# Spectral resampling, channel MLP and a selective scan on one core: TensorE work of the next sample moved and paired

## The reference

```python
def conv_ref(x, W1, b1, W2, b2, coef):      # layer 0
    xu = _upsample_rfft(xc)                 # band-limited, 64x64 -> 128x128
    h = h @ W1.T + b1                       # 96 -> 384 channels
    h = coef[:, 0] + coef[:, 1] * h + coef[:, 2] * (h * h)
    h = h @ W2.T + b2                       # 384 -> 96
    return _lpf_rfft(hc)[:, :, ::2, ::2]    # low pass, back to 64x64
...
def mamba(u, ...):                          # layer 1, L = 4096 steps in time
    xs, z = split(u @ W_in.T)               # 2 x 192 channels
    xc = silu(causal conv of 3 taps of xs)
    delta = softplus(dt @ W_dt.T + b_dt)    # dt, B, C = xc @ W_x.T
    h = exp(delta * A) * h + delta * B * xc # h: 192 channels x 16 states
    y = (h . C + xc * D) * silu(z)
    return y @ W_out.T
x = x + conv_ref(_gn(x), ...)
x = x + mamba(_gn(x), ...)
```

## Time and profile before

| what | us |
|---|---|
| median of 3 runs | 6282.98 (6277.81 to 6292.53) |
| the profiled execution, its own time | 6281.37 |
| its span, first to last instruction | 6279.6 |
| TensorE busy (modelled ends) | 6000.8, 96% of the span |
| VectorE busy | 5683.0, 90% |
| GpSimd busy | 5215.4, 83% |
| ScalarE busy | 5094.3, 81% |
| share of the 16 DMA engines' span | 66.3% |

### The profile page before, as it was taken

The page is one execution under the profiler, slowest core; times in us unless marked ns, Lnnn a source line. Parts: engine busy times, 40 slices in busy tenths (PEclk is TensorE's granted clock), DMA queues, the critical chain, the costliest instruction groups (busy, mean ns, idle before and its releaser), DMA issues. The chain is left out here.

```text
span 6279.6 us, 99521 instructions
## 1 busy us (share of the span) xinstructions
PE 6000.8 (96%) x32251; PEld 3116.7 (50%) x32251; DVE 5683.0 (90%) x4450; ACT 5094.3 (81%) x8658; POOL 5215.4 (83%) x5092
## 2 busy tenths in 40 slices
PE   8999999999999999999999999999999999998776
PEld 5645545454554545555455555545455454544222
DVE  0089999999999999999999999999999999999998
ACT  4588888888888888888888888888888888887664
POOL 0078888888888888888888888888888888888887
PEclk9999999999999999999999999999999999998665
DMA  3367676676767667676776767667676766766553
GB/s 95 89 167 174 161 172 155 168 166 165 172 156 169 158 168 169 160 180 145 173 162 161 175 156 180 150 167 166 163 171 163 171 158 164 167 147 157 131 118 75
DMA packets 805829, 983.27 MB, mean 157 GB/s; under 512 B 391259, under 2 KB 417543, under 8 KB 805319
## 3 DMA queue, kind: packets, MB, share of 16 engines
q1 hardware_dynamic: 805318, 976.92, 66.3%
HBM read 717.71 MB, written 259.00 MB: 156 GB/s over the span
## 5 line engine op out<-in xcount | busy, mean ns | idle before, releaser
L1183 POOL TENSOR_TENSOR hc<-hs,cs 128x512 f32<-128x512 f32 x3072 | 3840.8, 1273 | 631.0 <-DVE hs L1142 486.7
L1142 DVE TENSOR_TENSOR_SCAN hs<-av,state,b 128x512 f32<-128x512 f32 x2688 | 3257.6, 1263 | 84.0 <-DVE b L1136 1.8
L1008 ACT ACTIVATE av<-rep_d,nega 128x512 f32<-128x512 f32 x3072 | 2095.8, 713 | 33.2 <-DVE hs L1142 28.4
L1136 DVE TENSOR_TENSOR b<-rep_u,b 128x1536 f32<-128x1536 f32 x1024 | 1803.2, 1761 | 173.3 <-PE b L846 81.1
L855 PE MATMUL py<-hc,rsel 128*32 128x512 f32 x6144 | 1149.4, 638 | 12.5 <-POOL hc L1183 12.1
L769 PE MATMUL cb<-xu,w1a 96*128 96x392 f32 x2400 | 973.6, 509 | 0.9 <-ACT dlt L998 0.9
L774 PEld LDWEIGHTS cb<-w2c,g 128*98 128x98 f32 x9600 | 885.4, 167 | 147.1 <-issue 108.2
L774 PE MATMUL cb<-w2c,g 128*98 128x96 f32 x9600 | 908.0, 251 | 1.7 <-ACT g L956 1.7
L956 ACT ACTIVATE g<-cb,b1a 128x392 f32<-128x392 f32 x1200 | 680.3, 580 | 85.1 <-PE cb L769 76.7
L810 PE MATMUL cb<-xn,wtap 96*96 96x512 f32 x1536 | 721.9, 606 | 1.3 <-ACT xn L1029 1.0
L769 PEld LDWEIGHTS cb<-xu,w1a 96*128 96x128 f32 x2400 | 414.8, 190 | 373.8 <-issue 255.5
(11 more groups left out here) (109 smaller groups left out, 6674.1 us busy)
## 6 DMA issues: line engine op xcount, KB each, us to landing
rep_d<-delta_scratch SPq DMA_DIRECT2D x512, 384.0 KB, 7.3
rep_u<-deltax_scratch SPq DMA_DIRECT2D x512, 384.0 KB, 6.3
cs<-c_scratch SPq DMA_DIRECT2D x512, 256.0 KB, 5.9
delta_scratch<-dlt SPq DMA_DIRECT2D x128, 384.0 KB, 3.0
deltax_scratch<-dlt SPq DMA_DIRECT2D x128, 384.0 KB, 9.3
t1r<-t_scratch SPq DMA_DIRECT2D x160, 240.0 KB, 6.6
v_scratch<-v2s SPq DMA_DIRECT2D x192, 192.0 KB
xb<-in_x SPq DMA_DIRECT2D x128, 192.0 KB, 4.7
```

What stands on the lines that cost most here:

```text
L1008: act.activation(av[:, n % NAV, :], rep_d[:, k % 2, j, :], ACT.Exp, scale=nega[:, q, j:j + 1])\
L1136: dve.tensor_tensor(b3[:, 2::-1, :], of_hf[:, 2::-1, :], b3[:, 0:1, :].broadcast_to([128, 3, T]), ALU.mult).then_inc(dve_bu, 1)
L1142: dve.tensor_tensor_scan(hs[:, n % NHS, :], av[:, n % NAV, :], b3[:, n % 3, :], start, ALU.mult, ALU.add)\
L1183: pool.tensor_tensor(hc[:, n % NHC, :], hs[:, n % NHS, :], cs[:, k % 2, g % NQ, :], ALU.mult)\
```

## The change

SA and SB of a block become one item of the list. SA's code issues both products, one behind the other, into two neighbouring banks, after it has waited for both banks; SB's code issues nothing. The table of costs has 0.45 for each instead of 0.70. S ends at slot 78 (before: 87), and the steps at its end (SG1, SG2, WLD) move with it. The first part of W begins at slot 96 (105), its first two steps and WG nine slots earlier too, and it has 74 steps (72); the second part ends at slot 88 (87). The fillers fall from 48 to 10 a sample, since `warm` finds fuller groups.

```diff
 def s_steps():
     out = []
     for b in range(HH // XB_H):
-        out += [("ST", b), ("SA", b), ("SB", b)]
+        out += [(("ST", b),), (("SA", b), ("SB", b))]
     return out
...
-W_HEAD = 72
-S_LAST, W_FIRST, W_LAST, D_FIRST, D_LAST = 87, 105, 87, 100, 139
+W_HEAD = 74
+S_LAST, W_FIRST, W_LAST, D_FIRST, D_LAST = 78, 96, 88, 100, 139
...
-PE_US = {"ST": 0.45, "SA": 0.70, "SB": 0.70, "W_up": 0.70, "W_f": 0.71, "W_2": 2.10, "W_dn": 0.75, "D_lo": 1.20, "D_hi": 1.20,
+PE_US = {"ST": 0.45, "SA": 0.45, "SB": 0.45, "W_up": 0.70, "W_f": 0.71, "W_2": 2.10, "W_dn": 0.75, "D_lo": 1.20, "D_hi": 1.20,
...
-def even(steps, lo, hi):
+def even(groups, lo, hi):
     free = [p for p in range(lo, hi + 1) if p % NU not in KEEP_FREE]
-    return [(free[i * len(free) // len(steps)], st) for i, st in enumerate(steps)]
+    return [(free[i * len(free) // len(groups)], st) for i, steps in enumerate(groups) for st in steps]
...
-    return [st for p, st in stage_rows(True, True, False, False) if 90 <= p <= 140]
+    return [st for p, st in stage_rows(True, True, False, False) if S_LAST < p <= 140]
...
-                for bank_free, n_free in st.freed_all([i - RING] + [st.find(m, key) for m in made]):
+                before = [i - RING] + [i + 1 - RING] * (name == "SA")
+                for bank_free, n_free in st.freed_all(before + [st.find(m, key) for m in made]):
                     pe.wait_ge(bank_free, n_free)
...
-                elif name in ("SA", "SB"):
-
-                    r = int(name == "SB")
-                    half = slice(64 * r, 64 * r + 64)
-                    mm = pe.matmul(bank[0:GW, 0:4 * C], up_w[half, r, :],
-                                   xb[half, b % 2].rearrange("p i c -> p (i c)"), start=True, stop=True)
+                elif name == "SA":
+
+                    for r in range(2):
+                        half = slice(64 * r, 64 * r + 64)
+                        pe.matmul(cb[0:GW, (i + r) % RING, 0:4 * C], up_w[half, r, :],
+                                  xb[half, b % 2].rearrange("p i c -> p (i c)"), start=True, stop=True).then_inc(pe_conv, 1)
+                    return
+                elif name == "SB":
+                    return
```

More of the change, by code:

```diff
@@ L84, with single @@
 OFFSET = {"S": 2, "D": 1}
-def even(steps, lo, hi):
+def even(groups, lo, hi):
     free = [p for p in range(lo, hi + 1) if p % NU not in KEEP_FREE]
-    return [(free[i * len(free) // len(steps)], st) for i, st in enumerate(steps)]
+    return [(free[i * len(free) // len(groups)], st) for i, steps in enumerate(groups) for st in steps]
+def single(steps):
+    return [(st,) for st in steps]
 def loads(lo, hi, rows):
@@ L146, in stage_rows @@
     if d:
-        rows += [(DW_AT, ("DW", 0)), (D_FIRST - 6, ("DLD", 0)), (D_FIRST - 2, ("DG", 0))] + even(d_steps(), D_FIRST, D_LAST)
+        rows += [(DW_AT, ("DW", 0)), (D_FIRST - 6, ("DLD", 0)), (D_FIRST - 2, ("DG", 0))] + even(single(d_steps()), D_FIRST, D_LAST)
         rows += [(D_LAST + 5, ("DG1", 0)), (D_LAST + 10, ("DG2", 0))]
@@ L151, in stage_rows @@
     if w_head:
-        rows += [(S_LAST + 4, ("WLD", 0)), (W_FIRST - 3, ("WG", 0))] + even(w[:2], W_FIRST - 8, W_FIRST - 6)
+        rows += [(S_LAST + 4, ("WLD", 0)), (W_FIRST - 3, ("WG", 0))] + even(single(w[:2]), W_FIRST - 8, W_FIRST - 6)
         rows += level(w[2:W_HEAD], W_FIRST, NC8 * NU - 1, rows + list(beside))
@@ L186, in head_before @@
 def head_before():
-    return [st for p, st in stage_rows(True, True, False, False) if 90 <= p <= 140]
+    return [st for p, st in stage_rows(True, True, False, False) if S_LAST < p <= 140]
 def alone(*streams):
     rows = []
-    for steps in streams:
-        rows += [(i / len(steps), st) for i, st in enumerate(steps)]
+    for groups in streams:
+        rows += [(i / len(groups), st) for i, steps in enumerate(groups) for st in steps]
     return padded(rows)
@@ L400, in build @@
         N_SETUP = 12
-        BEFORE = [alone([("SLD", 0)] + s_steps() + [("SG1", 0), ("SG2", 0)]),
-                  alone([("WLD", 0), ("WG", 0)] + w_steps() + [("DW", 0)], [("SLD", 0)] + s_steps()),
-                  alone([("DLD", 0), ("DG", 0)] + d_steps() + [("DG1", 0), ("DG2", 0)], head_before()), plan_before()]
+        BEFORE = [alone(single([("SLD", 0)]) + s_steps() + single([("SG1", 0), ("SG2", 0)])),
+                  alone(single([("WLD", 0), ("WG", 0)] + w_steps() + [("DW", 0)]), single([("SLD", 0)]) + s_steps()),
+                  alone(single([("DLD", 0), ("DG", 0)] + d_steps() + [("DG1", 0), ("DG2", 0)]), single(head_before())), plan_before()]
         FIRST, FULL, TAIL, LAST = [plan_of(kind) for kind in ("first", "full", "tail", "last")]
```

## The result

The changed kernel takes 6213.63 us (median of 4 runs, 6210.52 to 6216.3) against 6282.07 for the kernel before in the same comparison (4 runs, 6277.81 to 6292.53): ratio 0.9888, 95% interval 0.9871 to 0.9906. The forecast was 6221, range 6206 to 6250. The profiled execution took 6212.51 with a span of 6210.6, 69.0 less than before's 6279.6.

The account below looks back on a forecast made before the run. Bound: VectorE, plus an unevenly filled TensorE. Savings of 49.4 (samples 1 to 13), 3.4 (sample 0), 0.3 (samples 14, 15) and 9 (prologue), 62.1 us, take 6281.4 to 6219.3; median 1.6 higher, 6221, range 6206 to 6250.

Parts of the forecast that it names:

- Bound and mechanism: Samples 1 to 13: VectorE needs 367.2 of 371.8 us; 4.6 are waits, in groups 20 to 27 and 45 to 48.
- The pair: SA and SB together take one SA, 0.82 us (bounds 0.77 to 1.64), saving TensorE 6.6 us a sample.
- The levelling: Scan groups: TensorE's work evened out, waits of 4.6 us a sample fall to 0.8, saving 3.8.
- The fillers: 38 fewer filler products a sample; they lay in TensorE's idle time, so priced at nothing.
- Rival 3: Fewer fillers let TensorE's clock fall in groups 28 to 34: 3 us a sample, 6263 us; chance 0.05.
- Sample 0: First sample of the scan: gains 3.4 us, as one wait, for the first x load, stays.
- Samples 14 and 15: Last two samples: 14 has no S, 15 nothing of the change; 0.3 us gained.
- Prologue: Before the scan: eight pairs give 6.6 us; first product at 317.4 to 318, 9 us earlier (bounds 2.8 to 11.7).
- 1: New start of W jams: 1.5 to 2.5 us a sample over the forecast's 0.4, 6236 to 6250 us; chance 0.15.
- 4: Slower: six W_f of slots 96 to 98 wait on late ScalarE, 5.7 us a sample, 6295 us; chance 0.04.
- 2: Pairs don't overlap at full clock: 0.2 us a sample in the scan, 6.6 in the prologue, 6231 us; chance 0.06.
- 5: All waits go, group 45 and start of W too, and prologue gains 11.7 us: 6207 us; chance 0.08.

Follow-up runs that it names:

- second run: Kernel before, SA and SB still apart, with the new slots and step counts: 6214.17 us, ratio 0.9884.
- fifth run: Changed kernel with the fillers' target at 5.3 instead of 4.8 us a group, 36 fillers a sample instead of 10: 6205.01 us, ratio 0.9871.
- sixth run: Changed kernel with fillers (target 4.8) also in sample 14, which has none in the changed kernel: 6212.69 us, ratio 0.9884.
- first: Changed kernel with its pairs kept but the old slots and step counts put back: 6226.18 us, ratio 0.9904.
- eighth: Kernel before, SA and SB apart, each reading all 128 partitions with zero weights for the other half: 6251.61 us, ratio 0.9943.
- seventh: Changed kernel with both filler edits, target 5.3 and fillers in sample 14 too: 6206.97 us, ratio 0.9874.
- third: Changed kernel with both products of a pair reading all 128 partitions, so they can't run side by side: 6216.62 us, ratio 0.9889.

## Why the prediction was right, and where its terms were off

**Bound and mechanism: right.** VectorE alone was put at 367.2 us a sample. The second run (new slots, no pairs) and the fifth (more fillers), without long dips of the clock, take 367.0 and 367.1, and the changed one's eleven undisturbed samples 366.5 to 367.5. The waits were mostly where the argument had them: 52 of the 104 in groups 20 to 27 and 39 at 45 to 48; 13 more, 5.9 us, stood at groups 2 to 7, which it doesn't name. They went with the unevenness of TensorE's work. That it was the unevenness and not the amount is shown by the second run: it takes no working step away, and clears them all. The waits to be had were 4.9 us a sample (371.9 less 367.0), where the prediction had 4.6.

**The pair: right in its own time, too small in what it saves.** 0.82 forecast, 0.823 the median of the 104 pairs of the samples behind the first. But phase 1, from its first W_up to DG, fell from 155.5 to 147.1 us, 8.4 where "eight pairs give 6.6". The step that failed is the count of the pair at one SA and nothing for the neighbours; the drains were mentioned as something that the rows could not tell apart, and left out of the sum. With 0.98 a pair it is 7.8.

**The levelling: right, its leftovers too large.** Of the 0.8 us a sample that was to stay (0.3 at group 45, 0.1 for av, 0.4 at the start of W) nothing stayed. At group 45 TensorE came in with slack. At the start of W the lead of ScalarE was enough: no W_f of groups 31 to 34 waited for it in any of the 13 samples. (TensorE's 12 waits for g, 3.1 us, all stand at group 7, in the second part of W.) What came in place of these 0.8 had no term in the sum: two samples of thirteen with 10 us of half clock, which take 3.2 and 3.0 us more than the same samples of the fifth run, 0.5 a sample over the thirteen. Net gain 4.4, forecast 3.8.

**The fillers: the step that was wrong.** "38 fewer: they lay in idle time, so nothing". Their time was free, but the clock was put at nothing. More of them are worth 5 to 8 us: the changed kernel and the fifth run differ by 5.2 us over samples 1 to 13, and the two stretches of 10 us at half clock, 6.2 us, account for it. That it is the 38 removed ones that were missing isn't shown: the second run has 12 and no long stretch, and the kernel before, with 48, falls to half clock for 3.4 us at group 32 in nine of its samples 1 to 13, at no cost. Rival 3 had the mechanism and the price (3 a sample where it strikes) and the place, groups 28 to 34; it struck in 2 samples of 13 and not in all, and with all the fillers gone it still cost 0.9 a sample over the floor of 367.0, not 3.

**Sample 0.** Forecast 3.4, measured 6.0. VectorE's waits for b and for a padding step's bank went from 9.2 us (6.8 and 2.4) to 3.1. I had let one of them stand whole, and it shrank as well, from 3.11 to 1.79.

**Samples 14 and 15.** Forecast 0.3 less, measured 3.9 more, nearly all of it in sample 14: its 6.8 us of waits for b against 2.9. Half clock fell on groups 39 and 44, with OUT and D in the one, X and D in the other. The mean clock of that sample hardly moved (0.84, before 0.85), only the place of the dips did. The sixth run shows that the clock is the cause of what the sample takes above 363.7. The dips move about from version to version (sample 14 takes 365.3, 369.2, 369.3, 370.2, 366.3, 363.7 and 367.7 in the first seven runs). They go with the slots: the three kernels with the old slots (before, first, eighth) take 365.0 to 365.4, the five with the new slots and no fillers in that sample 366.3 to 370.2. What places the dips is not known.

**Prologue.** First product forecast at 317.4 to 318, measured 316.89. The first DT was 13.9 us earlier (11.7 forecast; phase 1's further 1.8 is most of the rest). The stretch behind was off the other way: from DG to b it takes 1.8 us more than before, forecast 0.6 more; the wait for ScalarE that was to be filled there, 1.2 for dbc, is gone, but two others, 0.7 for dlt and 0.4 for xn, came in. The two errors nearly cancel, and that is luck.

**The tie of the second run.** It starts its scan 8.9 us later than the changed kernel and ends level: it gains 6.8 in samples 1 to 13 (4771.0 against 4777.8) and 1.5 in sample 0. It has no long dip:

```profile
693.63:5464.64 4771.01, 4686.65 (x25795) 2457.62 (x25792) 4605.71 (x3589) 4106.62 (x7034) 4233.66 (x4135) 1.00 0.72 167
```

Its TensorE does more work in the samples, 4686.65 busy against 4614.92. That TensorE's saved time is what let the clock fall fits with this and with the other runs that have fillers: the first, fifth and seventh (4683.94, 4684.38 and 4684.16 busy) have no long dip there, the third (4653.19) and the sixth (4615.76) have two each. It is argued from these sums, one trace of each kernel, and not shown for any one dip.

**Rivals.** 1 and 4 (the start of W jams): no wait for ScalarE there. 2: the pair's two products run side by side. 3 (the clock): see the fillers. 5 (everything goes): true of the waits, with 10.1 of the 11.7 us in the prologue; the clock took some of it back, and the fifth run, without long dips in samples 1 to 13, takes 6205, near this rival's 6207.

## What to carry to other kernels

When one engine sets the pace and another is nearly as full, look at the work between two hand-overs and not at the sum: moving steps to even it out gave the whole gain of the samples here, with no working step removed. Once the pace is reached, every us saved on the other engine counts only in stretches where that engine is alone (here phase 1), and may cost some of its clock elsewhere, so price the idle time that it leaves. Put products that use half of the array's rows side by side, or else give them full rows with zeros: alone they were the dearest form here.

## What the runs showed of the hardware

- A lone fp32 product of 384 columns on 64 rows takes 0.82 us to the next start, on all 128 rows 0.65, and it makes the steps on both sides of it 0.09 and 0.07 longer. A pair in different halves takes 0.82, two full-row ones in a row 1.29, and 1.37 to 1.39 beside a sum.
- Half clock for 3.4 us cost 0.2 us or less here, where TensorE has 2 us of slack (samples 4, 6 and 13 of the changed kernel against the same of the fifth run). For 10 us it cost 3.2 and 3.0 in the two samples of the changed kernel that have it, and 1.4 to 1.5 without the fillers in that stretch. In sample 2 the granted clock was 0.51, TensorE's 1.2 GHz, in the 10.3 us around the late groups and 1.00, its 2.4 GHz, right before and after; in the 9.70 us before it fell TensorE had been busy 9.06.
- Without any fillers, samples 1 to 13 still have a mean granted clock of 0.99, with TensorE busy 4619 of 4783 us.
